# A delta-rule transformer layer in fp32: the MLP's first tile and first weight pieces prepared inside the recurrence's last blocks

## The reference, cut to what matters

```python
x = x + 0.5 * ffn(layernorm(x))
# the block that the change touches:
r = layernorm(x)
h = rmsnorm(r, ln1_scale)
h = gdn_attention(h, ...)          # recurrence over the tokens: 16 heads of 32, then @ wo + bo
z = h + r
h = rmsnorm(z, ln2_scale)          # z * rsqrt(mean(z*z) + 1e-6) * ln2_scale
x = x + (gelu(h @ w1 + b1) @ w2 + b2 + z)
x = x + 0.5 * ffn(layernorm(x))
```

## Time and profile before

| | us |
|---|---|
| median of 3 runs (lowest, highest) | 3428.26 (3427.92, 3431.14) |
| the profiled execution | 3430.42 |
| its span | 3428.6 |
| PE busy | 3245.8 (95%) |
| DVE, ACT, POOL busy | 1836.5, 1309.6, 1191.1 |
| start of the recurrence, of the dense stage | about 992, 1761 |

### The profile page before, as it was taken

One profiled execution on the slowest core, in us unless ns is written; L12 is line 12 of the kernel. 1 busy time (PEld: TensorE's weight loads), 2 busy tenths in 40 slices (PEclk: granted clock), 3 DMA queues, 4 the chain that ended last, 5 costly groups with the idle time before them and its releaser, 6 DMA issues. The chain is left out here.

```text
span 3428.6 us, 150175 instructions
## 1 busy us (share of the span) xinstructions
PE 3245.8 (95%) x68430; PEld 2585.0 (75%) x68430; DVE 1836.5 (54%) x2956; ACT 1309.6 (38%) x2646; POOL 1191.1 (35%) x1209
## 2 busy tenths in 40 slices
PE   3999999999958999999989999999999999999997
PEld 2777777777747888888868777777777777777775
DVE  4778787878648888888223333323333323333332
ACT  3544444444313333333333333333333333333332
POOL 0335555555526666666101122202122211122220
PEclk7999999999969999999999999999999999999998
DMA  3354454545466776766640110010111010111000
GB/s 97 104 150 158 145 163 146 163 147 158 142 191 190 220 222 218 217 208 190 185 145 30 37 37 25 25 37 25 37 37 37 13 37 25 37 37 37 25 25 25
DMA packets 388817, 356.00 MB, mean 104 GB/s; under 512 B 58208, under 2 KB 321632, under 8 KB 385632
## 3 DMA queue, kind: packets, MB, share of 16 engines
q1 hardware_dynamic: 386352, 351.86, 33.1%
q10 hardware_dynamic: 2224, 0.90, 0.2%
HBM read 184.65 MB, written 153.09 MB: 99 GB/s over the span
## 5 line engine op out<-in xcount | busy, mean ns | idle before, releaser
L1835 DVE TENSOR_TENSOR glo<-gl,gh 128x512 fp32r<-128x512 f32 x256 | 195.0, 762 | 914.8 <-ACT gh L1740 914.7
L1736 ACT ACTIVATE gl<-bank,b1m 128x512 f32<-128x512 f32 x256 | 175.9, 687 | 782.4 <-PE bank L236 782.4
L234 PE MATMUL bank<-h_hi,w_hi 128*128 128x512 f32 x1024 | 425.1, 415 | 0.0
L234 PE MATMUL bank<-w_hi,gh 128*128 128x512 f32 x1024 | 409.5, 400 | 8.5 <-DVE glo L1835 8.5
L236 PE MATMUL bank<-h_hi,w_lo 128*128 128x512 f32 x1024 | 405.9, 396 | 0.0
L236 PE MATMUL bank<-w_hi,glo 128*128 128x512 f32 x1024 | 405.8, 396 | 0.0
L235 PE MATMUL bank<-h_lo,w_hi 128*128 128x512 f32 x1024 | 405.6, 396 | 0.0
L235 PE MATMUL bank<-w_lo,gh 128*128 128x512 f32 x1024 | 404.6, 395 | 0.0
L1221 PE MATMUL bank<-ringA 32*32 32x32 f32 x16512 | 242.4, 195 | 6.6 <-issue 5.5
L234 PEld LDWEIGHTS bank<-w_hi,gh 128*128 128x128 f32 x1024 | 192.3, 188 | 59.4 <-DVE glo L1835 15.4
L235 PEld LDWEIGHTS bank<-h_lo,w_hi 128*128 128x128 f32 x1024 | 192.9, 188 | 54.9 <-issue 10.8
(11 more groups left out here) (173 smaller groups left out, 7105.7 us busy)
## 6 DMA issues: line engine op xcount, KB each, us to landing
ringB<-heads_scratch SPq DMA_DIRECT2D x257, 192.0 KB, 2.7
ringA<-heads_scratch SPq DMA_DIRECT2D x260, 128.0 KB, 2.3
X<-in_L_attn_x SPq DMA_DIRECT2D x16, 1024.0 KB, 9.5
x_scratch<-X SPq DMA_DIRECT2D x16, 1024.0 KB, 4.5
heads_scratch<-vb SPq DMA_DIRECT2D x16, 1024.0 KB, 5.2
heads_scratch<-qk SPq DMA_DIRECT2D x16, 1024.0 KB, 6.7
heads_scratch<-kb SPq DMA_DIRECT2D x16, 1024.0 KB, 5.2
heads_scratch<-kbuf SPq DMA_DIRECT2D x16, 1024.0 KB, 7.2
```

The source lines that it names most:

```text
L234: e.matmul(o, lhs[0], rhs[0], start=first, stop=False)
L1736: e.activation(gl[k][:, :], bank[k][:, :], ACT.Gelu_apprx_tanh, bias=b1m[:, m:m + 1]).then_inc(a_gl, 1)
L1835: e.tensor_tensor(gh[k][1][:, :], gl[k][:, :], gh[k][0][:, :], ALU.subtract).then_inc(v_gl, 1)
```

## The change

It takes the preparation of the dense stage's first tile into the recurrence. In the recurrence's code:

- **SP**: at the end of blk 52's turn of the loop it loads z of tile 0 (1 MB, `Z0`), b1 (`b1m`) and b2 (`b2b`); at the end of blks 55 to 62 one 256 KB piece of w2 each. ln2_scale (`ln2`) is loaded at the start of the recurrence, behind `bo`.
- **ACT**: a `Square` at the end of the second chunk of blks 53 to 56 (the first waits for Z0), one rounding copy of a w2 piece in blks 57 to 59, and h_hi after its last `normalize`.
- **DVE/POOL**: mean and 1/rms in blk 57, the scaling in blks 58 to 61, h_lo between the last `low` and the last `add_out`.
- **PE**: 16 turns between the loop's last group and the last 12 products with wo. They go to banks 1, 3, 4, 5 (`TURN2`).
- **Dense**: PE, ACT, DVE and POOL start without waiting for `done2` (three of them wait for it at tile 1); SP still waits. `up` writes bank (m+1) % 2, so that `up(0, 0)` uses bank 1, and `up(0, 1)` waits for the last `add_out` to have read bank 0. DVE splits the lo parts of pieces 0 to 2 first.
- **Buffers**: Z0, H, h2 (hi and lo of h) and some small ones live through both stages; w1's staging lies in Z0, `lt` in h2; the rest is put in another order so that staging and w2 lie over buffers that the recurrence no longer reads. In the names of the changed kernel `h` is h_hi or h_lo, `Z<-in_L_attn_w` a piece of w1, and `H,ss` the square with its row sum.

```diff
@@ SP, start of the recurrence
             e.dma_start(bo[:, :], row(a["L0_attn_bo"], D)).then_inc(d_bo, 16)
+            e.dma_start(ln2[:, :], a["L0_attn_ln2_scale"].rearrange("(g p) -> p g", p=P), **SHORT).then_inc(d_bo, 16)
@@ SP, end of each block's turn
+                if blk == READY2:
+                    for i in range(2):
+                        e.wait_ge(d_z[i], 32)
+                    e.dma_start(Z0[:, :, :], z_v[0]).then_inc(d_x[0], 16)
+                    e.dma_start(b1m[:, :], a["L0_attn_b1"].rearrange("(g p) -> p g", p=P), **SHORT).then_inc(d_w3, 16)
+                    e.dma_start(b2b[:, :], row(a["L0_attn_b2"], D)).then_inc(d_w3, 16)
+                if READY2 + 2 < blk <= READY2 + 10:
+                    i = blk - READY2 - 3
+                    if i == 0:
+                        e.wait_ge(v_back, 4 * (NS - 1))
+                    elif i == 4:
+                        e.wait_ge(p_R, NC * (NS - 1))
+                    e.dma_start(stage3[i], pieces3[i][0]).then_inc(d_stage[i], 16)
@@ PE, after the loop            (READY2, TURN2 = 52, (1, 3, 4, 5))
             out_state(3)
             out_delta(3)
+            e.wait_ge(v_hs, 4)
+            for f in range(NF):
+                for b in range(NB):
+                    m = e.transpose(bank[TURN2[f]][:, b * P:(b + 1) * P], H[:, b, f * P:(f + 1) * P], ident)
+                m.then_inc(p_ht3, 1)
             e.wait_ge(v_olo, 2 * CHUNKS + 8)
             e.wait_ge(v_z, 2 * CHUNKS + 8)
             out_product(range(12))
@@ ACT
+                if at == 1 and READY2 < blk <= READY2 + NB:
+                    b = blk - READY2 - 1
+                    e.wait_ge(d_x[0], 16 * (NT // 2 + 1))
+                    e.activation(H[:, b, :], Z0[:, b, :], ACT.Square, accum_out=ss3[:, b:b + 1]).then_inc(a_ss, 1)
+                if at == 1 and READY2 + NB < blk <= READY2 + NB + AHEAD3:
+                    i = blk - READY2 - NB - 1
+                    e.wait_ge(d_stage[i], STAGED3[i] + 16)
+                    e.activation(pieces3[i][1], stage3[i], ACT.Copy).then_inc(a_whi3, 1)
...
             normalize(NBLK - 1)
+            e.wait_ge(d_bo, 32)
+            for f in range(NF):
+                e.wait_ge(p_ht3, f + 1)
+                e.activation(hT3[0][:, f, :], bank[TURN2[f]][:, :], ACT.Copy, scale=ln2[:, f:f + 1]).then_inc(a_hi3, 1)
@@ DVE
             low(CHUNKS // 2 - 1)
+            for f in range(NF):
+                e.wait_ge(a_hi3, f + 1)
+                e.scalar_tensor_tensor(hT3[1][:, f, :], bank[TURN2[f]][:, :], ln2[:, f:f + 1], hT3[0][:, f, :],
+                                       ALU.mult, ALU.subtract).then_inc(v_lo3, 1)
             add_out(NBLK - 1)
@@ PE, dense
-                bk, c = m % 2, slice(m * P, (m + 1) * P)
+                bk, c = (m + 1) % 2, slice(m * P, (m + 1) * P)
...
-            e.wait_ge(done2, 5)
-            for f in range(NF):
-                turn_h(0, f)
+            released[0] = v_z, 8 * NBLK + 16
@@ SP, dense
-            load_z(0)
-            ...
-            for i in range(NP3):
-                if i >= 8:
-                    e.wait_ge(v_wlo3, i - 8 + 1)
+            for i in range(8, NP3):
+                e.wait_ge(v_wlo3, i - 8 + 1)
                 e.dma_start(stage3[i % 8], pieces3[i][0]).then_inc(d_stage[i % 8], 16)
```

More of the change, by code:

```diff
@@ L1482, in dve_delta @@
                     e.wait_ge(a_w1hi, i + 1)
-                    e.tensor_tensor(pieces2[i][2], w1s[i % 2][:, :], pieces2[i][1], ALU.subtract).then_inc(v_w1lo, 1)
+                    e.tensor_tensor(pieces2[i][2], w1s[i % 2], pieces2[i][1], ALU.subtract).then_inc(v_w1lo, 1)
                 solver(c, 1)
+                if at == 2 and blk == READY2 + NB + 1:
+                    e.wait_ge(a_ss, 4)
+                    e.tensor_scalar(ss3[:, :], ss3[:, :], 1.0 / D, RMS_EPS, ALU.mult, ALU.add).then_inc(v_ms, 1)
+                if at == 2 and READY2 + NB + 2 <= blk < READY2 + 2 * NB + 2:
+                    b = blk - READY2 - NB - 2
+                    e.wait_ge(o_ms, 1)
+                    e.tensor_scalar(H[:, b, :], Z0[:, b, :], ss3[:, b:b + 1], None, ALU.mult).then_inc(v_hs, 1)
             add_out(NBLK - 2)
@@ L1530, in pool_delta @@
                 solver(c, 1)
+                if at == 3 and blk == READY2 + NB + 1:
+                    e.wait_ge(v_ms, 1)
+                    e.tensor_tensor(ss3[:, :], ss3[:, :], neg_half, ALU.pow).then_inc(o_ms, 1)
             add_bo(NBLK - 1)
         with ExitStack() as st:
[L1536 to L1543, removed]
             gl = [sbuf(st, f"gl{i}", [P, TOK]) for i in range(2)]
             gh = [(sbuf(st, f"gh{i}", [P, TOK], F32R), sbuf(st, f"glo{i}", [P, TOK], F32R)) for i in range(2)]
+            xT3 = sbuf(st, "x2T", [P, NF, TOK])
+            Z = [Z0, sbuf(st, "Z1", [P, NB, D])]
+            w2 = sbuf(st, "w2_hi", [P, NM, D], F32R), sbuf(st, "w2_lo", [P, NM, D], F32R)
             g3 = sbuf(st, "g3", [P, TOK])
@@ L1735, in gelu @@
                     e.wait_ge(v_gl, n - 1)
-                e.activation(gl[k][:, :], bank[k][:, :], ACT.Gelu_apprx_tanh, bias=b1m[:, m:m + 1]).then_inc(a_gl, 1)
+                elif n == 0:
+                    e.wait_ge(d_w3, SMALL3)
+                e.activation(gl[k][:, :], bank[1 - k][:, :], ACT.Gelu_apprx_tanh, bias=b1m[:, m:m + 1]).then_inc(a_gl, 1)
                 e.wait_ge(a_gl, n + 1)
@@ L1786, in ffn @@
                     relus(t, 4, 5, 6, 7)
[L1788 to L1794, removed]
             for t in range(NT):
+                if t == 1:
+                    e.wait_ge(done2, 5)
                 for m in range(NM):
```

51 lines of the change are left out of this document (25 added, 26 removed).

## The result

| | before | changed |
|---|---|---|
| median of 4 runs (lowest, highest), us | 3428.69 (3427.92, 3431.14) | 3384.92 (3384.3, 3387.23) |
| the profiled execution, its span | 3430.42, 3428.6 | 3387.23, 3385.4 |
| PE busy | 3245.8 (95%) | 3209.2 (95%) |

What follows compares the result with a forecast made beforehand. PE, busy 95% of the span, was taken as the bound, with a hole at the dense stage's start. 19.2 - 2.8 - 1.1 - 0.3 - 0.2 = 14.8 us gain, from 3428.26 to 3413.5; range 3408.7 to 3419.5.

Steps and rivals of the forecast that it cites:

- The head of the dense stage: From the recurrence's last group to the dense stage's second up product: PE's idle goes, `up(0, 1)` starts 19.2 us earlier.
- Rival D: Dense stage's start: something held covered delays it, 8 to 15 us stay on the path; 3424; chance 0.06.
- Z0 and the first square: Recurrence, blk 53: ACT's square waits for Z0's load, so PE waits 2.8 us, bounds 2.5 and 5.0.
- Rival A: Z0's load in the recurrence costs little; gain 17.5 to 19.5 us, 3409.5; chance 0.15.
- The clock behind it: Recurrence, after PE's wait for the first square: the lower clock costs 1.1 us, bounds 0 and 2.
- b1m and b2b: SP's queue after blk 52: ringB's load behind these two is just covered by Z0's wait; 0 us, bound 4.
- Rival B: Recurrence: the queue behind Z0 makes ringB's load some 4 us late, PE waits again; 3418.5; chance 0.16.
- Squares, copies, pieces: Recurrence's last blocks: ACT's four squares and three copies cost 0.3 us, bounds 0 and 0.8; w2 piece loads 0.
- Rival C: Recurrence's end: each of eight w2 pieces costs 2.49 us, 19.9 in all, so slower, 3433.4; chance 0.03.
- ln2: Start of the recurrence: loading 512 single elements behind lt and bo costs 0.2 us, bounds 0 and 2.

Runs made afterwards that it cites:

- e4: The changed kernel with Z0's load issued one block earlier, b1m and b2b left in place; 3383.93 us, ratio 0.9862.
- e2: The changed kernel, same instructions, order and banks, with four 32-byte pads so that up and down are at distance 32 instead of 0; 3409.65 us, ratio 0.9942.
- e3: The changed kernel with the pads of e2 except the last, so that only down is at distance 0 and up at 32; 3405.02 us, ratio 0.9929.
- e6: The changed kernel with pads around h2 and ahead of w2, up at distance 128 and down at 256; 3405.6 us, one run.
- e7: The changed kernel with pads around h2 and ahead of w2, up at distance 256 and down at 64; 3400.31 us, one run.
- e9: e4 plus a 352-byte pad ahead of the first stage's hT, with b1m, b2b and Z0 loaded at the ends of blks 38, 46 and 50; 3372.42 us.
- e5: The kernel before with one 928-byte pad ahead of b2b, up and down both at distance 0; 3397.23 us, ratio 0.9901.
- e1: The kernel before with a 32-byte pad ahead of b2b, up and down at distance 128 instead of 96; 3426.67 us, ratio 0.9991.
- e10: The kernel before with a 352-byte pad ahead of hT, first stage at distance 0 instead of 160; 3420.87 us, ratio 0.9973.

## Why the prediction was wrong

**The direction and the mechanism of the move were right; the time was wrong by a term that wasn't in the sum.**

- *The head of the dense stage*: predicted 19.2, measured 19.35. The turns took 1.97 (1.9 forecast), the restart and the 12 products came as worked out, nothing of ACT, DVE or the gelu chain was late, the clock stayed 1.00. Rival D is out.
- *Z0 and the first square*: PE's wait of 2.8 was measured as 2.81, and it is ACT's (2.98 for Z0, e4 takes it away with the load moved). Z0 took 5.47 from issue to square (1632.18 to 1637.65), 5.9 forecast; wherever something waited for this load, it took 5.5 to 6.1. The Trainium skill, "DMA: Bandwidth & Descriptors", section "Anatomy of one DMA — SWDGE (gpsimd) path", has a fit for the other way of issuing, and an estimate by it was 4.4; this case measures 5.47, and the measurement decides. Rival A is out.
- *The clock behind it* was mis-sized: predicted 1.1, bounds to 2. Blk 53 lost 5.2 in all, so 2.4 beside the wait, at a clock of 0.50 through the whole window from 1640 to 1644. With the wait gone (e4) the fall is gone. It was not the length of the wait that made the price. In e2 and e3, PE waited longer at this place (3.15 and 3.36), and the block lost only 1.5 and 1.4 beside the wait; in e6 and e7 (3.23 and 2.80) it lost 2.2 and 2.3. The clock was at full speed again by 1641 in e2 and by 1642 in e3, and only at about 1645 in the changed kernel. A window of e2, to be set beside the two of the changed kernel:

```profile
1638.00:1642.00 4.00, 4.00 (x150) 3.07 (x145) 0.00 (x0) 0.70 (x3) 0.00 (x0) 0.66 0.87 254
```

  So the one wait of the earlier trace rows showed the cheaper of two outcomes; what decides between them is open.
- *b1m and b2b*: the issue of 4.0 came (3.98) at the place foreseen and no wait for ringB of over a microsecond came with it. It came because Z0 stood right ahead, as Z did in the earlier trace rows; without a 1 MB load there it took 1.16 (e4) and 1.06 (e9). Rival B is out for the changed kernel; where Z0 no longer holds ACT, 1.1 and 0.4 of it show (e4).
- *Squares, copies, pieces*: the ten last blocks took 111.93, against 111.10 before, so 0.8 for 0.3. It holds over the traces: 111.9 to 112.2 in the eight with the change, 110.9 to 111.1 in the four without. Rival C would have had 20.
- *ln2*: 0.2 forecast. The 0.0 in the budget's first row hides it. From the last product of the first stage to the first `normalize` it is 67.5 to 68.7 in the four traces of before's order, 68.1 to 70.4 in the eight with the change, on the mean 1.1 more. Whether ln2 makes it, or the other places of the buffers, was not tested.
- **The step that failed**: under the change, front and diff say of the buffers that "the rest is put in another order", and the part-by-part costing has no entry for it. It was costed at nothing without a row or a word. It was worth about 25 us: e2 takes it away (3384.92 becomes 3409.65; by the ratios 0.0072, 24.7 us), and e5 gives it to the kernel before (33.9 us). That e5 gets more than e2 loses is in part the reference: before stands at 234.7 ns, e2 at 234.2, which is 3 us over 6,144 products. e5's products are also 0.4 ns closer than those of the changed kernel (2.5 us), and its steps from `up` to `down` and back are 5.8 ns shorter (2.2 us over the 373 in the trace; see below), less 1.6 of longer waits for `glo`. That makes 6 of the 9; the rest is within what executions differ by.

The prediction of the move by itself is thus tested by e2: 3409.65 against 3413.5, and 3 us of the difference are the 0.5 ns just named, not the move. Its trace has -19.4 at the head (`up(0, 1)` at 1765.73, behind a last `normalize` at 1758.43), +2.1 in the recurrence (723.14), +1.5 before it (1035.29), and -4.0 behind, which is its span of 3408.9 less 3428.6. That the total came near is in part luck: the recurrence itself differs by some microseconds from execution to execution. With the code of before it took 721.04, 717.65 (e1), 718.52 (e5) and 720.07 (e10), which is as large as the costs argued over.

What in the chip makes the distance count is open. That the stationary operand of the next product is loaded while the moving one streams, and that the two reads get in each other's way in the same partition, would fit, but is not shown. The traces have something on it at the seams, where a product of `up` is followed by one of `down` or the other way, so that the moving operand meets a stationary one of the other kind. In the changed kernel these two lie 128 apart, and the step over the seam is 232.6 ns on the mean, against 228.7 within a kind. In the kernel before they lie 0 apart, and it is 230.1 and 230.7, against 234.7. In e5, where all are 0 apart, it is 226.8. This speaks for the pair of what moves and what comes next; but in e6 the seam from `up` to `down` has distance 0 and 233.8, and in e2 it has 192 and 228.0, so that it isn't the whole rule. The order 0, 256, 64, then the rest was found and not explained. The direction made no difference where it was tried: `up` has the moving operand 96 ahead and `down` 96 behind before, at 234.7 each, and in e1 128 ahead and behind, at 234.0 and 234.1.

## What to carry to other kernels

When a change reorders buffers, treat the addresses as part of it: write down where the two operands of each hot product start, and compare mean durations of such products in the two traces before any stall is argued over; a percent on a bound engine is larger than most stalls. Here a pad of a few hundred bytes in two places (e5's and e10's) gives 33.9 and 9.5 us on the kernel before, more than the whole restructuring (about 20); and loads that something on the critical chain waits for are better issued some blocks ahead, apart from one another (e4's trace shows 3.3 us for the earlier load; the times of e4 and e9 are too near to those without it to confirm this).

## What the runs showed of the hardware

- The start-to-start time of 128x512 products with fp32r operands depended on the distance modulo 512 bytes per partition between stationary and moving operand: 228.2 to 228.9 ns at 0 for both kinds of product, 229.6 to 229.8 at 0 in the first stage, 229.7 to 230.0 at 256, 231.0 at 64, 233.6 to 235.2 at 32, 96, 128 and 160 (e3's `down`, at 0, had 230.2). At 96 and 128 it was the same with the moving operand ahead and behind.
- PE's waits of 2.81, 3.23 and 2.80 (the changed kernel, e6, e7) were followed by clock 0.50 and cost 2.4, 2.2 and 2.3 us beside themselves. Waits of 3.15 and 3.36 at the same place (e2, e3) cost 1.5 and 1.4, and one of 1.43 had cost about 1.1.
- On SyncE the issue behind the load of 2,048 single elements took 3.98, as 4.01 before, where a load of 1 MB stood right ahead of the two, and 1.16 (e4) and 1.06 (e9) where none did.
- A load of 1 MB issued from SyncE took 5.5 to 6.1 us from its issue to the operation that waited for it, over nine traces.
